# Two-layer dense model: TensorE's side steps (norm transposes, routers, q/k/v, key sums, states product) in later slots

## The reference, cut to what matters

```python
xn = layernorm(x)
x = x + attention(xn) * silu(ffn(xn))
```

```python
# attention: 16 heads of 8
Q, K = relu(rope(xn @ wq)), relu(rope(xn @ wk));  v = xn @ wv
out = (Q . cumsum(K x v)) / (Q . cumsum(K) + 1e-6);  s = out @ wo
# ffn: 8 experts of 352, top 2 of a softmax router, weights cw
h = silu(xn @ W1[e].T) * (xn @ W3[e].T)
y = sum_e cw[:, e] * (h @ W2[e].T)
```

## Time and profile before

| | us |
|---|---|
| median of 3 runs | 1460.89 (1455.99 to 1462.78) |
| the profiled execution's own time | 1474.24 |
| its span | 1472.0 |
| TensorE matmul busy | 1209.5 (82%) |
| VectorE busy | 951.6 (65%) |
| ScalarE busy | 614.2 (42%) |
| GpSimd busy | 554.7 (38%) |

### The profile page before, as it was taken

One profiled execution on the slowest core, in us unless ns is written; L12 is line 12 of the kernel. 1 busy time (PEld: TensorE's weight loads), 2 busy tenths in 40 slices (PEclk: granted clock), 3 DMA queues, 4 the chain that ended last, 5 costly groups with the idle time before them and its releaser, 6 DMA issues. The chain is left out here.

```text
span 1472.0 us, 21718 instructions
## 1 busy us (share of the span) xinstructions
PE 1209.5 (82%) x6688; PEld 680.1 (46%) x6688; DVE 951.6 (65%) x2613; ACT 614.2 (42%) x1293; POOL 554.7 (38%) x606
## 2 busy tenths in 40 slices
PE   5999998899989989898979886897866878777830
PEld 2443343334334333333334364586755666665620
DVE  4547668768658668568667552432956658597693
ACT  2433223224233232232222265784746557565720
POOL 0000530631621522503504413506665454465545
PEclk9999899999999999999999988997978889998965
DMA  9932002112102121120168378754655646566522
GB/s 296 319 161 86 31 28 86 38 35 79 38 30 80 36 79 35 39 81 22 36 186 248 97 215 227 222 172 138 196 160 158 193 127 201 165 182 180 151 82 57
DMA packets 155818, 183.63 MB, mean 125 GB/s; under 512 B 16621, under 2 KB 104237, under 8 KB 155078
## 3 DMA queue, kind: packets, MB, share of 16 engines
q1 hardware_dynamic: 139334, 148.83, 32.2%
q0 software_dynamic: 16384, 33.59, 7.9%
HBM read 83.79 MB, written 98.57 MB: 124 GB/s over the span
## 5 line engine op out<-in xcount | busy, mean ns | idle before, releaser
L1178 POOL DMA_INDIRECT y<-y_rows,idxy x256 | 264.6, 1034 | 241.1 <-issue 116.9
L1142 POOL DMA_INDIRECT rows<-xn,idx x256 | 251.8, 984 | 84.9 <-issue 80.7
L1013 ACT ACTIVATE hs<-GY 128x512 f32<-128x512 f32 x176 | 105.0, 597 | 331.2 <-PE GY L768 297.3
L768 PE MATMUL GY<-xn0T,wff 128*128 128x512 f32 x352 | 191.4, 626 | 0.0
L784 PE MATMUL ACC<-hs,wff 128*128 128x512 f32 x352 | 190.1, 629 | 0.0
L1122 POOL TENSOR_TENSOR ppause<-neg_half 128x1 f32<-128x1 f32 x64 | 13.4, 209 | 342.4 <-DVE idx L1472 232.2
L818 PE MATMUL U<-ident,xg 128*128 128x128 f32 x576 | 100.7, 302 | 46.0 <-ACT xT L1029 30.1
L1529 DVE TENSOR_TENSOR hs<-hs,B 128x512 f32<-128x512 f32 x96 | 65.7, 684 | 85.4 <-PE B L774 37.3
L1529 DVE TENSOR_TENSOR hs<-hs,U 128x512 f32<-128x512 f32 x80 | 54.9, 686 | 88.8 <-ACT hs L1013 57.4
L774 PE MATMUL B<-xw,wff 128*128 128x512 f32 (+2 forms) x304 | 102.8, 612 | 2.0 <-DVE hs L1529 1.6
L818 PEld LDWEIGHTS U<-ident,xg 128*128 128x128 f32 x576 | 69.8, 152 | 73.5 <-issue 59.8
(11 more groups left out here) (262 smaller groups left out, 2154.0 us busy)
## 6 DMA issues: line engine op xcount, KB each, us to landing
xg<-rows SPq DMA_DIRECT2D x144, 256.0 KB
y_rows<-ys SPq DMA_DIRECT2D x144, 256.0 KB
rows<-zero SPq DMA_DIRECT2D x2, 12288.0 KB, 47.0
rows<-zero SPq DMA_DIRECT2D x6, 2048.0 KB, 9.5
wd<-in_wd SPq DMA_DIRECT2D x1, 5120.0 KB, 24.7
wff<-in_w SPq DMA_DIRECT2D x3, 1408.0 KB, 9.2
rows<-xn,idx POOLq DMA_INDIRECT x256
y<-y_rows,idxy POOLq DMA_INDIRECT x256
```

Of the source, the lines that this page charges most:

```text
L768: nc.tensor.matmul(G[u % 2][:, :], w1_0[:, u * P:(u + 1) * P], xn0T[:], start=True, stop=True).then_inc(sem["g_ps"], 1)
L1013: nc.scalar.activation(hs[:, u % RH, :], G[u % 2][:, :], ACT.Silu).then_inc(sem["silu_ready"], 1)
L1142: pool.indirect_dma_start(rows, bass.IndirectOffsetOnAxis(ap=idx[:, t * 8 + k:t * 8 + k + 1], axis=0), xn1[:, t, :], None)\
L1178: pool.indirect_dma_start(y8[:, i % RG, k, :], None, y_d[0:groups * Q * P, :], bass.IndirectOffsetOnAxis(ap=idxy[:, b, t * 8 + k:t * 8 + k ...
```

## The change

The tables put most side steps of a batch one to three slots later. `xn1_T` goes from slot 9 to 11, `router1` from 12 to 14, `xn0_T` from 16 to 18, `router0` from 18 to 21, `rank` from 21 to 24, `qkv0` and `rope` each by one, `cum` and `outer` from 41 to 42, `qk_T` of tiles 0 and 1 by one; `scores_a` of the tiles by 2, 2, 1 and 1 slots. `place_d` and `norm0a` stay. `LAST_STEPS` keeps its own entries, but gets the attention's. The product of `kp` (the key sums) becomes a step `cum_k` of its own behind `outer`. In `s_scores_a` the states product goes ahead of the wait for `qm`. No instruction is added or taken out.

```diff
-ATTENTION = {40: ["kp"], 41: ["cum", "outer"], 42: ["den_a"], 43: ["states", "den_b"], 85: ["oT_copy"], 86: ["wo"], 87: ["s0"]}
+ATTENTION = {41: ["kp"], 42: ["cum", "outer", "cum_k"], 43: ["den_a"], 44: ["states", "den_b"], 85: ["oT_copy"], 86: ["wo"], 87: ["s0"]}
+TILE0 = (46, 56, 65, 75)
...
-    for at, name in ((32 + 2 * t, "qkv0"), (33 + 2 * t, "rope"), (45 + 10 * t, "qk_T"), (46 + 10 * t, "qkT_copy"),
-                     (49 + 10 * t, "scores_a"), (50 + 10 * t, "mask_a"), (51 + 10 * t, "scores_b"), (52 + 10 * t, "mask_b"),
-                     (54 + 10 * t, "av")):
+    for at, name in ((33 + 2 * t, "qkv0"), (34 + 2 * t, "rope"), (TILE0[t], "qk_T"), (TILE0[t] + 1, "qkT_copy"),
+                     (TILE0[t] + 5, "scores_a"), (TILE0[t] + 6, "mask_a"), (TILE0[t] + 7, "scores_b"), (TILE0[t] + 8, "mask_b"),
+                     (TILE0[t] + 9, "av")):
...
-STEPS = {0: ["res_silu"], 1: ["res_gate"], 3: ["res_T"], 4: ["res_add"], 6: ["res_norm"], 9: ["xn1_T", "res_r1"],
-         10: ["xn1T_copy"], 11: ["norm0a"], 12: ["router1"], 13: ["probs1"], 14: ["norm0b"], 15: ["topk1a"],
+STEPS = {0: ["res_silu"], 1: ["res_gate"], 3: ["res_T"], 4: ["res_add"], 6: ["res_norm"], 9: ["res_r1"], 11: ["xn1_T", "norm0a"],
+         12: ["xn1T_copy"], 14: ["router1"], 15: ["probs1", "norm0b"], 17: ["topk1a"], 18: ["xn0_T"], 19: ["xn0T_copy"],
...
                 nc.tensor.matmul(V[:, P:2 * P], onesf[:], qk[:, 1, 0, :], start=False, stop=False, skip_group_check=True)
+
+            def s_cum_k(t):
                 pe.wait_ge(*seen.next("kp_ready"))
...
             def s_scores_a(t):
                 pe.wait_ge(*seen.next("qkT0_ready"))
-                pe.wait_ge(*seen.next("qm_ready"))
-                reuse("X0")
                 reuse("V")
                 nc.tensor.matmul(V[:, t * P:(t + 1) * P], states[:, t, :], qkT[:, 0:P], start=(t == 0), stop=False, skip_group_check=True)
+                pe.wait_ge(*seen.next("qm_ready"))
                 score(0, "X0")
                 score(1, "X1")
```

More of the change, by code:

```diff
@@ L133 @@
         ITEM_CW[e] = len(ITEM_UP) + len(ITEM_CW)
-ATTENTION = {40: ["kp"], 41: ["cum", "outer"], 42: ["den_a"], 43: ["states", "den_b"], 85: ["oT_copy"], 86: ["wo"], 87: ["s0"]}
+ATTENTION = {41: ["kp"], 42: ["cum", "outer", "cum_k"], 43: ["den_a"], 44: ["states", "den_b"], 85: ["oT_copy"], 86: ["wo"], 87: ["s0"]}
+TILE0 = (46, 56, 65, 75)
 for t in range(T):
-    for at, name in ((32 + 2 * t, "qkv0"), (33 + 2 * t, "rope"), (45 + 10 * t, "qk_T"), (46 + 10 * t, "qkT_copy"),
-                     (49 + 10 * t, "scores_a"), (50 + 10 * t, "mask_a"), (51 + 10 * t, "scores_b"), (52 + 10 * t, "mask_b"),
-                     (54 + 10 * t, "av")):
+    for at, name in ((33 + 2 * t, "qkv0"), (34 + 2 * t, "rope"), (TILE0[t], "qk_T"), (TILE0[t] + 1, "qkT_copy"),
+                     (TILE0[t] + 5, "scores_a"), (TILE0[t] + 6, "mask_a"), (TILE0[t] + 7, "scores_b"), (TILE0[t] + 8, "mask_b"),
+                     (TILE0[t] + 9, "av")):
         ATTENTION.setdefault(at, []).append((name, t))
-STEPS = {0: ["res_silu"], 1: ["res_gate"], 3: ["res_T"], 4: ["res_add"], 6: ["res_norm"], 9: ["xn1_T", "res_r1"],
-         10: ["xn1T_copy"], 11: ["norm0a"], 12: ["router1"], 13: ["probs1"], 14: ["norm0b"], 15: ["topk1a"],
-         16: ["xn0_T"], 17: ["xn0T_copy"], 18: ["topk1b", "router0"], 19: ["exp0"], 20: ["topk1c"], 21: ["rank"],
-         22: ["place_a"], 25: ["place_b"], 27: ["place_c"], 31: ["place_d"], 35: ["place_e"], 39: ["place_f"], 40: ["scatter"],
-         44: ["table"], 50: ["topk0a"], 62: ["topk0b"], 75: ["cw0_T", "cw0T_copy"]}
+STEPS = {0: ["res_silu"], 1: ["res_gate"], 3: ["res_T"], 4: ["res_add"], 6: ["res_norm"], 9: ["res_r1"], 11: ["xn1_T", "norm0a"],
+         12: ["xn1T_copy"], 14: ["router1"], 15: ["probs1", "norm0b"], 17: ["topk1a"], 18: ["xn0_T"], 19: ["xn0T_copy"],
+         20: ["topk1b"], 21: ["router0"], 22: ["exp0", "topk1c"], 24: ["rank"],
+         25: ["place_a"], 27: ["place_b"], 29: ["place_c"], 31: ["place_d"], 36: ["place_e"], 40: ["place_f"], 41: ["scatter"],
+         45: ["table"], 51: ["topk0a"], 63: ["topk0b"], 76: ["cw0_T", "cw0T_copy"]}
 LAST_STEPS = {0: ["res_silu"], 1: ["res_gate"], 3: ["res_T"], 4: ["res_add"], 6: ["res_norm"], 9: ["xn1_T", "res_r1"],
@@ L152 @@
     for t in range(T):
-        table.setdefault(47 + 10 * t, []).append(("weights_a", t))
-        table.setdefault(54 + 10 * t, []).append(("weights_b", t))
+        table.setdefault(48 + 10 * t, []).append(("weights_a", t))
+        table.setdefault(55 + 10 * t, []).append(("weights_b", t))
     for at, names in ATTENTION.items():
```

## The result

The changed kernel takes 1474.07 us (median of 22 runs, 1456.38 to 1500.95), the kernel before, run beside it, 1462.19 us (22 runs, 1445.36 to 1481.56). The ratio is **1.007, 95% interval 1.0041 to 1.0100**: slower by 0.7%, some 10 us, where 6 us faster was forecast. Its profiled execution took 1478.98 us with a span of 1476.6. Ratios compare undisturbed runs only; where the kernel before takes over 1460 us the runs of one kernel lie up to 3.5% apart, so ratio and medians can differ there.

What follows compares the result with a forecast made beforehand. Part one was taken as held by a chain through VectorE and TensorE, part two's waits by signals held until GpSimd's scatters end. Gains of 2 us (tile 0 and before) and 4 (tiles 1 to 3): 1460.9 - 6 = 1455, range 1450 to 1461.

Steps and rivals of the forecast that it cites:

- the second rival: Slots 34 to 40, ScalarE between the ropes: 1.7 us longer in each of six batches, 10 us, 1471; chance 0.18.
- Slots 9 to 33, nothing: Steps up to place_d: VectorE's idle time 2.75 us against 2.79, so place_d ends when it did.
- Slots 33 to 42, 0.4 lost: The four ropes: 2 x 0.5 us new idle time less 0.61 filled; cum starts 0.4 us late.
- The clock at `cum`, put at nothing: At cum no half-speed cost was counted; half-speed stretches were named only for part two's waits of 2.4 us.
- Six batches: Tile 0 and before: 0.35 us gained a batch, counted over 6 batches, 2 us.
- Slots 42 to 54, 0.4 gained back: From cum into tile 0: key sums' 0.76 us wait goes, qk_T waits 0.3, a further item covers 0.45.
- Tiles 1 to 3, 4 us: Part two: held signals move the waits for qm; 0.7 us x 7 = 5, of which 4 us taken as gain.
- The sign of being right: Part one still 47 to 48 us, key sums' wait gone; part two's wait moved, about the same length.
- waits close: TensorE's waits in part one close: 25 us, so 1436; with half the qm waits, 1424; chance 0.27.

Runs made afterwards that it cites:

- e4: Changed kernel with two buffers rr used in turn by the ropes; 1393.7 us, ratio 1.0050 to the kernel before.
- e6: Changed kernel, unchanged, profiled again on a chip of the slower kind; 1479.1 us against 1473.9 for the kernel before, ratio 1.0105.
- e13: Kernel before, unchanged, profiled on a chip of the quicker kind; 1386.2 us, ratio 0.9998.
- e14: Changed kernel, unchanged, on a chip of the quicker kind; 1403.6 us against 1385.6 for the kernel before, ratio 1.0113.
- e15: Changed kernel with av of tiles 0 and 2 one slot later, one buffer rr; 1399.5 us, ratio 1.0101 to the kernel before.
- e9: Kernel before with place_e moved behind kp, place_f and the scatters behind qn, nothing of the change; ratio 1.0050 to the kernel before.
- e10: Changed kernel with two buffers rr and av of tiles 0 and 2 one slot later; 1382.6 us, ratio 0.9977 to the kernel before.
- e18: Same kernel as e10, run again on a chip with late signals; median 1474.5 us, ratio 0.9957 to the kernel before.
- e16: e10 with the key sums (cum_k) ahead of outer again; ratio 1.0065 to the kernel before.

## Why the prediction was wrong

**The sign.** 1455 was forecast, 1474 came. Of the cases named the second rival is the nearest, ScalarE between the ropes, 1471 in all. That its number is so near is in part luck. It had 1.7 us lost a batch, because nothing of VectorE's old idle time would be saved. Most of it was saved, and a batch lost 1.0 to `cum`; the rest came from TensorE's clock and from batches 0 and 7, which stood in no case's sum. Point by point:

- **Slots 9 to 33, nothing.** Nearly right. Of VectorE's idle times 1.15, 0.9 and 0.7 were foreseen and 1.13, 0.99 and 0.78 came:

```profile
337.82 0.32 DVE L1377 MAX8 m<-pp 128x8 f32<-128x160 f32 x1 [1.13 <-issue]
...
339.81 0.69 DVE L1531 TENSOR_TENSOR hs<-hs,B 128x512 f32<-128x512 f32 x1 [0.99 <-ACT hs L1015]
...
344.84 0.32 DVE L1407 TENSOR_TENSOR runn<-run,V 128x160 f32<-128x160 f32 x1 [0.78 <-PE V L736]
```

  TensorE waits 0.56 at `rank`, as described, though the profile names no engine that ends this wait. `place_d` ended 0.33 us late, not 0.
- **Slots 33 to 42, 0.4 lost. The first step that failed.** Two waits of 0.57 came, as described, and `hs` of unit 8 filled the old idle time. But from the first rope to the last it took 7.98 us and not 7.34, 0.64 more where 0.4 was counted, and `place_d`'s 0.33 came on top. So `cum` is 1.0 us late and not 0.4, 7.3 us over the eight batches where 0.4 x 6 = 2.4 were counted. e4 takes 0.8 of the 1.0 back by the second `rr`.
- **The clock at `cum`, put at nothing. The second step that failed.** I charged the waits in part two with half speed and did not ask what a wait that grows from 0.35 to 2.2 us (the ropes' 1.0, and the gaps closed ahead of it) would do: 3 x 1.7 = 5 us in this profile, five such stretches in e6.
- **Six batches.** Batches 0 and 7 were left out. On the chip of e13 and e14 they cost 2.3 us (93.75 less 91.48 from one start to the next) and 3.1 us (46.41 + 6.55 + 45.57 against 44.58 + 5.39 + 45.44), 5.4 of the 15.7.
- **Slots 42 to 54, 0.4 gained back.** The key sums' wait went, `qk_T` waits 0.58 and not 0.3. And I had counted the items around `av`, not the slots between it and the mask: two before, one after. That is 0.9 us a batch (e15).
- **Tiles 1 to 3, 4 us.** Right that the waits would move: to the states product for `qkT` (5.1), to a `W3` product (3.3) and to the scores (3.4 + 2.2). With 14.0 in all against 24.9 they did not keep their length. Part two is 9.7 and 14.5 us shorter in the two pairs of profiles with late signals, 2.5 of it the broadcast's shift, and 1.5 longer on a chip without them, where the kernel before has no wait for `qm` to win back. What the gain is worth in plain runs is not shown.

So in the profiles the chain's 7 to 8 us, the clock's 5 and the late `qn` and `av` outweigh what part two gives back. The sign of being right, part one at 47 to 48 us, failed with 50.3 and 48.7 in batches 3 and 4. The rival "waits close" fell as argued against it. The Trainium skill (Perfetto Trace Analysis, Optimization Strategy) says to find what each gap of the engine to be optimized waits for and to let that start sooner or end faster, which is more than the "remove its gaps" of the prediction. The change did neither and moved the waiting steps later. The trace agrees that this is not enough: 11.8 us of gaps before the `xn` transposes and `router0` closed, and 12.1 more opened at `cum`. A gap whose cause is another engine's chain only moves along it.

## What to carry to other kernels

When a table of slots moves steps on one engine, write out what stands between the moved steps on the others: a product that falls out from between two users of one buffer turns into a wait, and a second buffer (e4) gives it back. Count the slots between a producer and its consumer before and after, and every batch that uses the table, the first and the last too. A wait in front of matrix products that grows, here from 0.35 to 2.2 us, may be paid twice, the second time by TensorE's clock. Before a step is moved later, look for the next writer of what it reads: in e9 that was the next batch's `xn`.

## What the runs showed of the hardware

- The same kernel takes 1386 us on three chips and 1462 to 1474 on the others, 5 to 6% more (each chip used in one session). In layer 0 the difference sits in the stretches with indirect DMAs on GpSimd: 367 against 413 us in part two of the kernel before, 0.1 us from a batch's start to `cum` in batches 1 to 6. The second stage takes 585 to 599 us on the one kind and 627 to 645 on the other, over all kernels. On the slower kind ScalarE's copies in part two start up to 3.9 us (kernel before) behind the recorded end of TensorE's transposes, mostly just ahead of the end of a group of four scatters.
- The same wait of 2.21 us is followed by half speed in some batches and not in others of one execution (e14: in batch 3, not in 4 to 6). Single waits of some 1.4 us before `cum` were never followed by it (e4, e10, e18), but waits of 1.42 and 0.76 some 2 us apart five times in six (e16).
